# First stage of a fused two-layer kernel: nibbles in three transfers of 128 rows, and a new wait ahead of the gathers of zeros

## What is computed

```
y      = x @ W.T + 2 * sum_e gates[e] * (x @ A[e].T) @ B[e].T    # gates: softmax over the top 2 of 8 router logits
wq     = (qweight_gu >> shifts) & 15                             # packed 4-bit weights, 512 x 2752
zq     = ((qzeros_gu >> shifts) & 15) + 1                        # packed 4-bit zeros, 4 groups
w_gu   = scales_gu[g_idx] * (wq - zq[g_idx])
h      = silu(y @ w_gu[:, :1376]) * (y @ w_gu[:, 1376:])
x      = x + h @ w_down                                          # w_down is quantized in the same way
```

## Time and profile before

| | us |
|---|---|
| median of 3 runs (444.53 to 444.99) | 444.74 |
| the profiled execution | 445.29 |
| its span, first to last instruction | 443.5 |
| TensorE busy | 439.6 |
| VectorE busy | 345.6 |
| GpSimd busy | 192.8 |

### The profile page before, as it was taken

One profiled execution on the slowest core, in us unless ns is written; L12 is line 12 of the kernel. 1 busy time (PEld: TensorE's weight loads), 2 busy tenths in 40 slices (PEclk: granted clock), 3 DMA queues, 4 the chain that ended last, 5 costly groups with the idle time before them and its releaser, 6 DMA issues.

```text
span 443.5 us, 5522 instructions
## 1 busy us (share of the span) xinstructions
PE 439.6 (99%) x1954; PEld 358.9 (81%) x1954; DVE 345.6 (78%) x446; ACT 218.2 (49%) x285; POOL 192.8 (43%) x162
## 2 busy tenths in 40 slices
PE   8999999999999999999999999999999999999997
PEld 4688888888888888888888888888888888888886
DVE  3778999898876988949787668768688578999922
ACT  4514575665542212528577656456466554474200
POOL 0356888987007200900005869897997400000000
PEclk9999999999999999999999999999999999999999
DMA  8955112210007686287369617937568146885623
GB/s 272 227 165 175 52 49 80 86 48 0 2 1 254 205 314 256 82 303 304 119 238 327 241 47 225 338 125 267 182 210 273 60 144 262 342 292 182 217 105 142
DMA packets 30456, 79.98 MB, mean 180 GB/s; under 512 B 2384, under 2 KB 15840, under 8 KB 28768
## 3 DMA queue, kind: packets, MB, share of 16 engines
q1 hardware_dynamic: 26752, 68.24, 44.4%
q0 software_dynamic: 3104, 10.73, 8.0%
q10 hardware_dynamic: 576, 0.72, 0.5%
HBM read 58.95 MB, written 20.72 MB: 180 GB/s over the span
## 4 chain that ended last, share of the span: by engine, by line
PE 99%; DVE 0%; issue 0%; DVEq 0%
PE ps L1670 10%; PE ps L1930 10%; PE ps L1932 10%; PE ps L1931 10%; PE ps L1671 10%; PE ps L1674 10%; PE ps L2045 5%; PE ps L2044 5%; PE ps L1790 5%; PE ps L1792 5%; PE ps L1791 5%; PE ps L2043 5%; PE ps L1913 2%; PE ps L1911 2%; PE ps L1912 2%; PE ps L1681 1%
## 5 line engine op out<-in xcount | busy, mean ns | idle before, releaser
L1670 PE MATMUL ps<-h_hi,ring_hi 128*128 128x512 f32 x152 | 59.4, 391 | 0.0
L1671 PE MATMUL ps<-h_lo,ring_hi 128*128 128x512 f32 x152 | 59.2, 389 | 0.0
L1110 DVE TENSOR_TENSOR ring_lo<-raw,ring_hi 128x1792 fp32r<-128x1792 f32 (+3 forms) x24 | 47.1, 1966 | 11.1 <-ACT ring_hi L746 11.0
L1930 PE MATMUL ps<-zt_hi,ring_hi 128*128 128x512 f32 x140 | 54.6, 390 | 0.0
L1932 PE MATMUL ps<-zt_hi,ring_lo 128*128 128x512 f32 x140 | 54.5, 389 | 0.0
L1931 PE MATMUL ps<-zt_lo,ring_hi 128*128 128x512 f32 x140 | 54.5, 389 | 0.0
L746 ACT ACTIVATE ring_hi<-raw 128x1792 fp32r<-128x1792 f32 (+1 forms) x23 | 36.6, 1593 | 23.5 <-PE ps L1932 10.1
L1674 PE MATMUL ps<-h_hi,ring_lo 128*128 128x512 f32 x152 | 47.8, 389 | 0.0
L636 POOL DMA_INDIRECT scale<-in_sc_gu,idx_gu x20 | 27.6, 1380 | 23.6 <-DVE idx_dn L1147 16.6
L1670 PEld LDWEIGHTS ps<-h_hi,ring_hi 128*128 128x128 f32 x152 | 28.5, 188 | 6.7 <-issue 0.5
L1674 PEld LDWEIGHTS ps<-h_hi,ring_lo 128*128 128x128 f32 x152 | 28.5, 188 | 6.0
(11 more groups left out here) (252 smaller groups left out, 1111.1 us busy)
## 6 DMA issues: line engine op xcount, KB each, us to landing
ad_raw<-in_w1T SPq DMA_DIRECT2D x8, 1024.0 KB, 5.9
wd<-down_weights SPq DMA_DIRECT2D x7, 1024.0 KB, 5.6
down_weights<-dhi SPq DMA_DIRECT2D x7, 896.0 KB, 4.6
down_weights<-dlo SPq DMA_DIRECT2D x7, 896.0 KB, 4.0
raw<-in_gu SPq DMA_DIRECT2D x12, 512.0 KB, 3.6
wd<-down_weights SPq DMA_DIRECT2D x7, 768.0 KB, 5.6
draw<-in_d SPq DMA_DIRECT2D x7, 512.0 KB, 4.3
dn_work<-in_qw_dn SPq DMA_DIRECT2D x11, 256.0 KB
```

The lines of the kernel that those rows point to most:

```text
L1110: dve.tensor_tensor(dst, src, hi_part.bitcast(F32), ALU.subtract).then_inc(done_sem, 1)
L1670: pe.matmul(ps[:, bank + hf, :], w_hi, v_hi[:, t], start=first, stop=False)
L1671: pe.matmul(ps[:, bank + hf, :], w_hi, v_lo[:, t], start=False, stop=False)
L1930: pe.matmul(ps[:, bank, :], ring1_hi[s][:, w], z_hi[:, t], start=first and k == 0, stop=False, skip_group_check=True)
```

## The change

SyncE loads the nibbles in three transfers, each over all 128 partitions and over 4, 4 and 3 of the 11 tiles' columns, and the array in DRAM holds the 64 rows twice for that. On GpSimd a wait for s_gex, which VectorE sets with the gates' expansion, is put after the wait for the store of the zeros and ahead of the four gathers of zeros. The nibble count of VectorE's wait follows the number of transfers.

```
+        NIB_LOADS = ((0, 4), (4, 8), (8, FT0))
...
-            for hp in range(2):
-                sp.dma_start(nib[64 * hp:64 * hp + 64, :].bitcast(U32), a["qw_gu"]).then_inc(s_qw, 16)
+            for i0, i1 in NIB_LOADS:
+                w = slice(2 * P * i0, 2 * P * i1)
+                sp.dma_start(nib[:, w].bitcast(U32), a["qw_gu"][:, w]).then_inc(s_qw, 16)
...
             pool.wait_ge(s_zk, 16)
+            pool.wait_ge(s_gex, 1)
             for k in range(KD):
                 gather(zg[:, 4 * ZW * k:4 * ZW * (k + 1)], kept_z, idx_gu[:, 0, k:k + 1], s_zg)
...
-            dve.wait_ge(s_qw, 32)
+            dve.wait_ge(s_qw, 16 * len(NIB_LOADS))
...
-        "qw_gu": np.ascontiguousarray(qg.transpose(0, 2, 1, 3)).view(np.uint8)...,
+        "qw_gu": np.concatenate([qb, qb]),
```

More of the change, by code:

```diff
@@ L2121 @@
     qg = pad_f(v["L0_ffn_qweight_gu"]).reshape(64, 2, FT0, P)
+    qb = np.ascontiguousarray(qg.transpose(0, 2, 1, 3)).view(np.uint8).reshape(64, FT0, 2 * P, 4).transpose(0, 1, 3, 2).reshape(64, -1).view(np.uint32)
     sg = pad_f(v["L0_ffn_scales_gu"]).reshape(G_GU, 2, FT0, P)
@@ L2148 @@
         "bT": v["L0_cond_B"].transpose(0, 2, 1).reshape(E * R, D)[:, order],
-        "qw_gu": np.ascontiguousarray(qg.transpose(0, 2, 1, 3)).view(np.uint8).reshape(64, FT0, 2 * P, 4).transpose(0, 1, 3, 2).reshape(64, -1).view(np.uint32),
+        "qw_gu": np.concatenate([qb, qb]),
         "sc_gu": sc_rows[:2 * NPAIRS].reshape(NPAIRS, 2, G_GU, 2 * P).transpose(0, 2, 1, 3).reshape(NPAIRS * G_GU, 4 * P),
```

## The result

| | median, us | runs | ratio to before, 95% interval |
|---|---|---|---|
| before | 444.83 | 6 (444.34 to 445.02) | |
| changed | 446.58 | 6 (446.08 to 446.87) | 1.0041 [1.0029, 1.0052] |

The change makes the kernel slower by 1.75 us. The forecast was 445.2 with a range of 444.4 to 446.0, so both the size and the verdict "no change that can be measured" were wrong; the result lies on rival 2's side. The profiled execution took 446.86 us with a span of 445.1.

The account below looks back on a forecast made before the run. TensorE was taken as the bound, held by a slackless chain from gathers of zeros through VectorE. Nibbles -0.0, start +0.66 and instructions -0.11 gave +0.5 us on 444.74: 445.2 us, range 444.4 to 446.0.

Parts of the forecast that it names:

- rival 2: Slower by over 0.2%: first two gathers' descriptor writing locked out beside b_lo and nibbles, up to 446.8 us; chance 0.16.
- The start: First gather of zeros on GpSimd, released by VectorE's expansion, starts at 27.24, 0.66 us later than before.
- The base: Chain from gathers of zeros through VectorE to TensorE's quantized tiles has no slack, so TensorE loses the full 0.55 us.
- The four instructions: GpSimd's four gathers of zeros take 4.38 us in sum, 0.11 less than before, the first taking 1.38.
- The landing: VectorE starts adding zeros 3.28 us after the last gather instruction, as before.
- This holds wherever the store lands: The first gather's 0.66 us delay stands whenever the store of zeros lands, since the later semaphore counts.
- Zeros at 35.8, TensorE at 44.9: Expected signs: VectorE's first addition of zeros near 35.8 us, TensorE's load of the first quantized tile near 44.9.
- The nibbles: Wider SyncE load lands nibbles some 6 us sooner, around 19 us, well above 196 GB/s; worth 0.0 us.
- In the kernel with only this half: With the wide load but no wait, GpSimd's gathers of zeros could start near 23.2 us, 3.4 us sooner.
- it gives the kernel none by itself, because nobody stands waiting for nibbles: The wide load alone brings no gain: VectorE reads nibbles first at 27.49, directly behind b_lo, without a wait.
- Rival 3: Faster: wider load removes TensorE's 0.4 us x-tile stop, 444.9 us; chance 0.06 within 0.2%, 0.08 for more.
- Rival 4: Load gets no faster, store lands as before at 26.3 us, same +0.5 us; shares the forecast's chance of 0.58.

Follow-up runs that it names:

- experiment 3: Kernel before, without the wait, its two 64-row nibble transfers each reading their own half of a doubled DRAM array: 445.03 us, ratio 1.0011.
- s_hg: Changed kernel with GpSimd's new wait moved later, to the semaphore VectorE sets behind the gates' multiply: 452.33 us, ratio 1.0170.
- experiment 12: Wide load alone, without the new wait, plus four tiny writes at the end of VectorE's program: 448.33 us, ratio 1.0096.

## Why the prediction was wrong

Two steps failed, the price of the wait's start and the base that it was added to. To see both, the rows have to be counted from the same piece of TensorE's work, the load of the logits' transposes (at 20.19 to 20.96 us in these traces), and not from the start of the span:

| us from that load to | expansion | first gather of zeros | zeros added | first quantized tile |
|---|---|---|---|---|
| before, the trace of the prediction | 5.37 | 5.67 | 14.36 | 23.48 |
| before, second trace | 5.52 | 2.56 | 11.42 | 23.19 |
| before, doubled array (experiment 3) | 5.37 | 4.02 | 12.35 | 23.19 |
| changed | 5.38 | 6.85 | 15.61 | 24.75 |
| changed, second trace | 5.38 | 6.85 | 15.59 | 24.75 |
| wait alone | 5.39 | 6.85 | 15.71 | 24.83 |
| changed, nibble instructions late | 5.38 | 6.85 | 14.77 | 23.98 |
| changed, wait on s_gate_c | 5.37 | 4.06 | 12.51 | 23.20 |

**The start, the larger error.** The sum had "+ 0.66 (start)". Against its own execution the first gather moved by 1.18 us (5.67 to 6.85). The expansion did not move, as forecast: it is 5.4 us behind TensorE's load in both kernels. But GpSimd resumed not 0.26 us after it but 0.78. It was 0.77 to 0.78 in all kernels where VectorE released a gather of zeros (the wait alone, s_hg, s_gate_c, the nibble instructions late, and both traces of the changed kernel); the 0.26 had been taken from a gather of scales, which starts sooner and then takes 1.69. That is 0.52 us too little. In times from the span's start the forecast of 27.24 seems met, by 27.30, but this is luck: in the trace of the changed kernel all of TensorE's and VectorE's work stands 0.46 us sooner there, and the stop of 0.41 us for the x tile is absent. It is absent from the second trace of before and from that of the wait alone too, so this is no gain of the change.

**The base.** "Nothing in it has slack, so what the gathers of zeros lose, TensorE loses" was read from one execution in which the store of zeros released the gathers at 26.58. In the second trace of before they start at 23.15, and VectorE has 2.4 us to spare. The wait moves the first gather by 4.15 us (23.15 to 27.30) there and TensorE only by what exceeds the slack, 1.56 us by the table. In the trace of the prediction 0.29 of these were spent already (23.48 against 23.19). I had written that this execution stood 0.55 us above the median and carried that difference through as a constant; 0.61 us of its distance to the second trace lie in this stage, 0.32 ahead of TensorE's load (20.91 against 20.59) and 0.29 behind it, which the wait's own delay contains. That about 23.2 is the usual place without the wait is inferred from the three traces in the table that have it; most executions left no trace.

**The four instructions**: 4.38 predicted, 1.67 + 0.95 + 0.95 + 0.94 = 4.51 measured. The first meets more of the nibble instructions than the 1.38 that I took for it; the bound of 1.98 held. The landing followed the last by 3.34 us, not 3.28. Together 0.19 us too little.

In sum: 0.55 forecast, 0.52 for the start, 0.29 for the base and 0.19 for the instructions and the landing make 1.55 of the 1.75 us measured. The last 0.2 are not placed. Either of the two larger errors alone would have left the time at 445.8 us or below, inside the range of 444.4 to 446.0.

**"This holds wherever the store lands"** was half right. The start of the gathers in the changed kernel does not depend on the store, but the distance to before does.

**Rival 2** named the nibble instructions' lock-out and put 446.8 as its end. Its time was nearly right, but its condition, a sum of 4.73 us or more for the four instructions, was not met (4.51). Moving the nibble instructions away gave back 0.8 us of the 1.75, since with the slack gone each part of the delay counts; the trace of the prediction had nearly the same excess in its own gathers (0.69 us against 0.72), so it can't be what was missing from the sum.

**Zeros at 35.8, TensorE at 44.9**: 36.06 and 45.20, off by 0.3 us from the span's start, and by 0.7 us when counted from TensorE's load (1.25 and 1.27 us later than in its own execution, where 0.55 was forecast).

**The nibbles**: around 19 us at a rate well above 196 GB/s, and a low one behind: as forecast, and worth nothing by themselves in the changed kernel, since the wait alone has the same ratio. "In the kernel with only this half" the gathers did start near 22.4 (forecast 23.2), but the step "it gives the kernel none by itself, because nobody stands waiting for nibbles" left out a loss: that kernel is the slower of the two halves. The new wait shields the changed kernel from that, and costs 1.75 us for it.

**Rival 3**: the early stop of 0.41 us at 11 us was absent after the change, but it was absent from the second trace of before as well; so the load earned nothing there. **Rival 4** is excluded by the windows (394 GB/s from 13 to 16 us).

**A better version?** None was found. With s_gate_c in place of s_gex the changed kernel is at 1.0004 [0.9995, 1.0013] of before: it repairs the loss, and since TensorE has no stop at this place in the typical execution of before, there is nothing here to win.

## What to carry to other kernels

Ask for a second execution before calling a chain free of slack: a wait that ends with a DMA's landing moves by microseconds between executions of one kernel, and a profiled time above the median can come from the very stage under study. Count the rows of two traces from the same piece of work on the engine that binds, not from the start of the span. Take the price of a wait's release from the same kind of instruction. Before adding a wait, find the latest harmless start of what it holds (here 34.5 us for the addition of zeros) and put the wait where it keeps that, as s_gate_c does and s_gex does not. A single profile in which a stall has vanished proves nothing until it is repeated.

## What the hardware showed that was not expected

- The store of zeros released the gathers at 26.58 in one execution of the kernel before and at 23.15 in another, with the same program: 8.4 and 6.0 us after it was issued.
- A gather that waited for VectorE starts 0.78 us after the release when its source is the array of zeros and takes 0.95 us with nothing beside it; a gather of scales starts 0.26 to 0.28 us after it and takes 1.15 to 1.69. What makes the difference was not tested.
- While GpSimd issued gathers back to back in the load-only kernels, VectorE's short instructions came with gaps of up to 1.22 us (experiment 12), though not in every trace, and in six of seven traces of the load-only kernels VectorE was idle ahead of an instruction whose inputs from TensorE were there, until 33.7 to 34.6 us (3.9 us at the longest where the nibble instructions stood ahead of it). The stretch goes when the scales' gathers are held back, and nothing tried explains it.
- After TensorE had been out of work for 2.6 to 2.8 us (the load alone) the granted clock was 0.57 to 0.65 over the next 4 us in three traces and 1.00 in others with stops of 1.9 to 2.75; after 5.6 us it was 0.57.
